# Joining the projections and the local attention of an image in one stage, with the root's steps and the loop's last copies moved

## The reference

```python
q = x @ wq.T                                   # x = layernorm(h), 16 heads of 64
k, v = split(x @ wkv.T)                        # one head each
q = _rmsnorm(_rope(q), q_norm_w)               # over the 64 features of a head
k = _rmsnorm(_rope(k), k_norm_w)
mask = (cols <= rows) & (rows - cols <= 128)
scores = where(mask, einsum(q, k) / sqrt(64), -1e30)
attn = softmax(scores)
h = h + (attn @ v).reshape(..., 16 * 64) @ wo.T
```

## Time and profile before

| | |
|---|---|
| median of 3 runs | 976.79 us (975.57 to 984.98) |
| profiled execution | 969.34 us, span of the core 967.1 us |
| mean granted clock of PE | 0.897 of full |
| busy, share of the span | PE 77%, PEld 50%, DVE 65%, ACT 46%, POOL 40% |
| first product of `project`, images 1 to 4 | 56.75, 187.00, 317.11, 449.77 us |
| first exponential of `windowed` | 98.41, 228.64, 361.16, 491.40 us |

### The profile page before, as it was taken

The page is one execution under the profiler, slowest core; times in us unless marked ns, Lnnn a source line. Parts: engine busy times, 40 slices in busy tenths (PEclk is TensorE's granted clock), DMA queues, the critical chain, the costliest instruction groups (busy, mean ns, idle before and its releaser), DMA issues. The chain is left out here.

```text
span 967.1 us, 21086 instructions
## 1 busy us (share of the span) xinstructions
PE 747.3 (77%) x8204; PEld 482.5 (50%) x8204; DVE 630.0 (65%) x1210; ACT 443.2 (46%) x1389; POOL 383.2 (40%) x432
## 2 busy tenths in 40 slices
PE   5577999887998879998769989978899965302870
PEld 5232677434775326774257744864577732201650
DVE  0378788596886787876968847676677728500890
ACT  0022899234995228991369935213666610200210
POOL 0035466254663445662646622652000000074475
PEclk9999999998999889999979999988999977655875
DMA  8144000080000620000300000008000021014200
GB/s 287 59 174 83 2 3 2 21 238 2 3 2 1 210 49 1 4 2 1 84 2 3 2 2 1 2 1 111 2 2 2 2 78 43 1 52 102 50 20 13
DMA packets 59992, 41.60 MB, mean 43 GB/s; under 512 B 51744, under 2 KB 57340, under 8 KB 59108
## 3 DMA queue, kind: packets, MB, share of 16 engines
q1 hardware_dynamic: 57446, 33.03, 13.7%
q10 hardware_dynamic: 144, 4.19, 1.1%
q0 software_dynamic: 2304, 3.04, 1.0%
HBM read 25.44 MB, written 7.15 MB: 34 GB/s over the span
## 5 line engine op out<-in xcount | busy, mean ns | idle before, releaser
L770 ACT ACTIVATE work<-ps,small,rq 128x160 f32<-128x160 f32 x512 | 243.1, 487 | 54.2 <-DVE small L719 53.7
L749 POOL TENSOR_TENSOR work<-work,small 128x512 f32<-128x512 f32 x128 | 133.3, 1042 | 138.1 <-DVE small L733 138.1
L716 DVE TENSOR_REDUCE ps<-ps 128x4 f32<-128x640 f32 x128 | 106.5, 832 | 52.4 <-PE ps L639 52.1
L727 DVE COPY pT<-ps 128x640 f32<-128x640 f32 x128 | 105.4, 823 | 8.2 <-PE ps L652 7.9
L770 ACT ACTIVATION_READ_ACCUMULATOR work<-ps,small,rq 128x1 f32 x512 | 105.2, 206 | 0.0
L1441 POOL DMA_INDIRECT sent_rows<-big,xb x32 | 30.9, 966 | 182.4 <-DVEq L1393 173.0
L639 PE MATMUL ps<-kT,big 64*128 64x160 f32 x1024 | 102.6, 322 | 0.0
L269 PE MATMUL ps<-xT,s_proj_w 64*128 64x512 f32 x288 | 78.9, 661 | 21.5 <-DVE prod L581 13.2
L669 PE MATMUL ps<-pT,vwin 128*64 128x128 f32 x1024 | 84.2, 282 | 10.6 <-ACT big L758 2.4
L609 POOL TENSOR_TENSOR big<-prod 128x1024 f32<-128x1024 f32 x28 | 66.4, 2372 | 47.5 <-DVE prod L581 47.0
L639 PEld LDWEIGHTS ps<-kT,big 64*128 64x128 f32 x1024 | 80.3, 200 | 0.4
(11 more groups left out here) (275 smaller groups left out, 1361.2 us busy)
## 6 DMA issues: line engine op xcount, KB each, us to landing
xb<-in_x SPq DMA_DIRECT2D x3, 4096.0 KB, 12.7
xb<-in_x ACTq DMA_DIRECT2D x1, 4096.0 KB, 15.1
vrem<-hl SPq DMA_DIRECT2D x64, 64.0 KB, 2.2
sent_rows<-empty_row SPq DMA_DIRECT2D x8, 325.0 KB, 10.0
s_proj_w<-in_proj_w SPq DMA_DIRECT2D x1, 1536.0 KB, 6.5
big<-sent_rows SPq DMA_DIRECT2D x5, 264.0 KB, 5.1
big<-sent_rows SPq DMA_DIRECT2D x5, 256.0 KB, 4.6
xb<-in_ffn_w SPq DMA_DIRECT2D x1, 1028.0 KB, 4.9
```

Source lines behind the costliest of these rows:

```text
L716: ch.step(v.tensor_reduce(row_max(c), ps[:, s_banks(c), 0:2 * SPAN].rearrange("p e (h k) -> p e h k", h=2), X, ALU.max))
L727: v.tensor_copy(pT[:, c % 2, :].rearrange("p (q r t) -> p r q t", r=2, t=D), ps[:, 4:6, 0:(NQ + 1) * D].rearrange("p r (q t) -> p r q t", ...
L749: g.tensor_tensor(probs[:, c % 3, :, 0:P], probs[:, c % 3, :, 0:P], bc(small[:, c % 4, 3, :], P), ALU.mult)
L770: nc.scalar.activation(probs[:, c % 3, q, :], bank[2 * (c % 2) + e][:, SPAN * hh:SPAN * hh + SPAN], ACT.Exp, bias=small[:, c % 4, 1, q:q + ...
```

## The change

The two stages of an image become one, so that only PE, DVE, ACT, POOL and SP's own semaphores stand between them; a second chain semaphore and names of their own for three counters go with it. `K_SUMS` and the steps after it move: the sums to step 4, the values to 5, the `ones` products to 7 and 8, `kT` after step 9. `STEPS` stays in order, so (8, 0) is step 16. The four transposes of the sums go to four places in `work` with no addition between; after the last, two `tensor_scalar` add the epsilon to the whole of `rq`, then the root follows. The second sums use banks 0 and 1. Token products at the end of the projections are one, and five before chunk 2. In the last three chunks DVE copies half of `pT` and ACT the other half.

```diff
-        K_SUMS, K_VALUES, K_NORMS, K_SCALED = 3, 4, (8, 9), 10
+        K_SUMS, K_VALUES, K_NORMS, K_SCALED = 4, 5, (7, 8), 9
-        SUM_BANKS = ((7, 6), (2, 3))
+        SUM_BANKS = ((7, 6), (0, 1))
-        LATE_TOKENS = 3
+        LATE_TOKENS = 1
-        STEPS[-3], STEPS[-2] = STEPS[-2], STEPS[-3]
+        VALUE_LOADS = 2 * NQ - 1 + NQ * NQ
...
-        sums_turned = pTr_own[:].rearrange("p a n -> p (a n)")
+        sums_turned = work[:].rearrange("p (k n) -> p k n", k=4)
-                v.memset(rms_eps[:], D * RMS_EPS)
... PE, project
-                        pe.wait_ge(S["prod_done"], UNITS - 1)
+                        pe.wait_ge(S["prod_done"], UNITS - 2)
... ACT, project
-                    if s == K_VALUES:
+                    if s == K_VALUES - 1:
... DVE, project
-                        ch.step(v.transpose(sums_turned, bank[SUM_BANKS[hh][w]][:]))
-                        v.sem_inc(S["q_root"], 1)
-                        ch.step(v.tensor_tensor(rq[:, w * CHUNKS // 2:(w + 1) * CHUNKS // 2, :, hh],
-                                                sums_turned.rearrange("p (c e) -> p c e", e=32)[:, :, 0:2],
-                                                rows(rms_eps[:].to_broadcast([P, 2]), CHUNKS // 2), ALU.add))
+                        v.transpose(sums_turned[:, 2 * hh + w, :], bank[SUM_BANKS[hh][w]][:]).then_inc(S["q_root"], 1)
...
                 q_sums(1)
+                v.wait_ge(S["q_root"], 4)
+                for hh in range(2):
+                    ins = v.tensor_scalar(rq[:, :, :, hh], sums_turned[:, 2 * hh:2 * hh + 2, :].rearrange(
+                        "p w (c e) -> p (w c) e", e=32)[:, :, 0:2], D * RMS_EPS, None, ALU.add)
+                ch.step(ins)
                 one_over_root(v, ch, rqflat, rqflat)
... between project and windowed
+        SHARED_FROM = CHUNKS - 3
+        def turned_half(c, r):
+            return pT[:, c % 2, :].rearrange("p (q r t) -> p r q t", r=2, t=D)[:, r]
+        def bank_of_half(r):
+            return bank[4 + r][:, 0:(NQ + 1) * D].rearrange("p (q t) -> p q t", t=D)
... PE, windowed: turn(c) and values(c) wait by this instead of pT_ready alone
+                def turned_kept(c):
+                    pe.wait_ge(S["pT_ready"], c + 1)
+                    if c >= SHARED_FROM:
+                        pe.wait_ge(S["pTr_ready"], c + 1 - SHARED_FROM)
...
+                pe.wait_ge(S["prod_done"], UNITS)
+                pe.wait_ge(S["square_done"], len(PAIR_ORDER))
+                pe.wait_ge(S["rot_done"], len(PAIR_ORDER))
                 for n in range(CHUNKS + 4):
+                    if n == 0:
+                        pe.wait_ge(S["q_root"], 4)
...
-                    if n == 4 and b + 1 < IMAGES:
-                        pe.wait_ge(S["h_ready"], 1)
+                    if n == 4:
+                        pe.wait_ge(S["x_loaded"], 16 * VALUE_LOADS)
+                        if b + 1 < IMAGES:
+                            pe.wait_ge(S["next_kept"], 1)
... DVE, windowed
-                        v.tensor_copy(pT[:, c % 2, :].rearrange("p (q r t) -> p r q t", r=2, t=D),
-                                      ps[:, 4:6, 0:(NQ + 1) * D].rearrange("p r (q t) -> p r q t", t=D)).then_inc(
-                                          S["pT_ready"], 1)
+                        if c < SHARED_FROM:
+                            v.tensor_copy(... the same ...)
+                        else:
+                            v.tensor_copy(turned_half(c, 0), bank_of_half(0)).then_inc(S["pT_ready"], 1)
... ACT, windowed
                 for c in range(CHUNKS - 4, CHUNKS):
+                    if c + 1 < CHUNKS:
+                        a.wait_ge(S["transposed"], c + 2)
+                        a.wait_ge(S["pv_done"], c)
+                        nc.scalar.activation(turned_half(c + 1, 1), bank_of_half(1), ACT.Copy).then_inc(S["pTr_ready"], 1)
                     outputs(c)
...
-            stage(lambda block: project(block, b))
-            stage(lambda block: windowed(block, b))
+            stage(lambda block: (project(block, b), windowed(block, b)))
```

More of the change, by code:

```diff
@@ L127, in program @@
         moe_b2 = sb("moe_b2", [P, E * D], BF16)
-        first_guess, rms_eps = sb("first_guess", [P, 1]), sb("rms_eps", [P, 1])
+        first_guess = sb("first_guess", [P, 1])
         ones, ones_mean, zeros = sb("ones", [P, P]), sb("ones_mean", [P, P]), sb("zeros", [P, P])
@@ L200, in program @@
             "v_dve", "kprod", "scores_done", "bias_ready", "exp_done", "scaled", "transposed",
-            "pT_ready", "pTr_ready", "tokens_kept", "tokens_turned", "pv_done", "oT_ready", "wo_done", "sums_inverted",
+            "pT_ready", "pTr_ready", "tokens_kept", "tokens_turned", "out_done", "out_kept", "next_kept", "loop_chain", "pv_done", "oT_ready", "wo_done", "sums_inverted",
             "zero_done", "slots_ready", "pool_chain", "sent", *(f"back{k}" for k in range(CHUNKS_X)), "turned_back", "hid_act",
@@ L557, in _ @@
                         n += 1
-                sp.wait_ge(S["x_loaded"], 16 * n)
+                sp.wait_ge(S["x_loaded"], 16 * VALUE_LOADS)
                 if b + 1 < IMAGES:
@@ L647, in turn @@
                     if c >= 1:
-                        pe.wait_ge(S["pT_ready"], c)
+                        turned_kept(c - 1)
                     for q in range(NQ + 1):
@@ L655, in values @@
                 def values(c):
-                    pe.wait_ge(S["pT_ready"], c + 1)
+                    turned_kept(c)
                     if c >= 1:
@@ L694, in _ @@
                                                oT[:, p, w * HALF:(w + 1) * HALF], start=(p == 0), stop=(p == PAIRS - 1))
-                ins.then_inc(S["proj_done"], 1)
+                ins.then_inc(S["out_done"], 1)
                 if b + 1 < IMAGES:
                     turn_normed(pe, 1)
-                pe.wait_ge(S["v_act"], 1)
+                pe.wait_ge(S["out_kept"], 1)
                 turn_halves(outT, 3, S["wo_done"])
@@ L702, in _ @@
             def _(v):
-                ch = Chain(v, S["dve_chain"])
+                ch = Chain(v, S["loop_chain"])
                 for n in range(CHUNKS + 3):
@@ L711, in _ @@
                         v.wait_ge(S["tokens_turned"], 1)
+                        v.wait_ge(S["h_ready"], 1)
                         v.tensor_copy(h_next.rearrange("p (w j) d -> p j w d", w=2),
-                                      bank[6][:].rearrange("p (j w d) -> p j w d", w=2, d=D)).then_inc(S["h_ready"], 1)
+                                      bank[6][:].rearrange("p (j w d) -> p j w d", w=2, d=D)).then_inc(S["next_kept"], 1)
                     if c < CHUNKS:
@@ L726, in _ @@
                             v.wait_ge(S["pv_done"], c - 1)
-                        v.tensor_copy(pT[:, c % 2, :].rearrange("p (q r t) -> p r q t", r=2, t=D),
-                                      ps[:, 4:6, 0:(NQ + 1) * D].rearrange("p r (q t) -> p r q t", t=D)).then_inc(
-                                          S["pT_ready"], 1)
+                        if c < SHARED_FROM:
+                            v.tensor_copy(pT[:, c % 2, :].rearrange("p (q r t) -> p r q t", r=2, t=D),
+                                          ps[:, 4:6, 0:(NQ + 1) * D].rearrange("p r (q t) -> p r q t", t=D)).then_inc(
+                                              S["pT_ready"], 1)
+                        else:
+                            v.tensor_copy(turned_half(c, 0), bank_of_half(0)).then_inc(S["pT_ready"], 1)
                     c = n - 1
@@ L734, in _ @@
                 if b + 1 < IMAGES:
-                    v.wait_ge(S["h_ready"], 1)
+                    v.wait_ge(S["next_kept"], 1)
                     layernorm(v, ch, h_next, xn_in_order, tmp, moe, st, TILES)
@@ L774, in _ @@
                 for c in range(CHUNKS - 4, CHUNKS):
+                    if c + 1 < CHUNKS:
+                        a.wait_ge(S["transposed"], c + 2)
+                        a.wait_ge(S["pv_done"], c)
+                        nc.scalar.activation(turned_half(c + 1, 1), bank_of_half(1), ACT.Copy).then_inc(S["pTr_ready"], 1)
                     outputs(c)
-                a.wait_ge(S["proj_done"], 1)
-                nc.scalar.activation(outT, bank[0][:], ACT.Copy).then_inc(S["v_act"], 1)
+                a.wait_ge(S["out_done"], 1)
+                nc.scalar.activation(outT, bank[0][:], ACT.Copy).then_inc(S["out_kept"], 1)
                 if b + 1 < IMAGES:
```

## The result

The changed kernel takes 935.07 us (934.44 to 941.04), the kernel before 976.18 (974.29 to 984.98): ratio 0.958, interval 0.954 to 0.962. Two more comparisons on other chips gave 0.967 (0.963 to 0.972) and 0.959 (0.957 to 0.962). The forecast was 945, 32 us less; 41 were measured. On the chip with 0.967 the two medians are 968.4 and 939.3, 29 us apart. The profiled execution took 934.44, span 932.6, against 969.34 and 967.1: the span is 34.5 less.

A forecast was written before the change was run, and what follows sets the result against it. ACT's exponentials bound the loop's steady part, no engine the projections. Terms gave 8.5 us in images 1 to 3 and 6.4 in image 4, 31.9 in all, taken off the median 976.79: 945, range 935 to 950, chance 0.66.

The forecast's parts named there:

- keys' root a pass later: Projections: one more product ahead of the keys' root and DVE's waits for projections gone; gain 2.5 us an image.
- first pair of additions: Projections: two transposes in DVE's product queue without their chained additions; gain 1.1 us an image, bounds 0.8 and 1.2.
- second pair: End of projections: second sums to rq by a transpose and two TENSOR_SCALAR; gain 1.4 us an image, bounds 0.3 and 1.7.
- order of the last steps: End of projections: (8,0) at step 16 makes the second sums one product later; minus 1.1 us an image.
- one stage: Projections to attention: no barrier, scores ready while DVE is in the root; gain 2.7 us, bounds 1.2 and 2.8.
- token products, clock: Before chunk 2: five token products at full clock, exponentials sooner; gain 2.1 us in images 1 to 3, none in 4.
- loop's end: Last three chunks: ACT's half of the pT copy stands ahead of its outputs; minus 0.2 us an image.
- the root waits for the port: Rival, end of projections: new sums wait for POOL's last rotation, 1.4 us not gained in four images; 951, chance 0.06.
- Image 4: Whole fourth image, which has no next tokens and so no token-product gain: forecast gain 6.4 us.
- the rival for a slower result: Attention loop's passes fall to 1.2 GHz, 1.7 us more per cold pass; 1% slower from 25 of 128; chance 0.03.

The follow-up runs named there:

- krate: Kernel before with only the keys' sums, values, norms and kT moved to steps 4, 5, 7, 8 and 9: 959.4 us, ratio 0.989.
- added: Changed kernel with the four chained additions behind the transposes again and none at the end: 948.6 us, ratio 0.972.
- swapped: Changed kernel with steps 15 and 16 exchanged again, (8,0) first: 940.7 us, ratio 0.963.
- best: Changed kernel with DVE alone copying pT and five unread products on PE in image 4 before chunk 2: 934.9 us, ratio 0.958.
- warm: Kernel before with unread products on PE behind the projections' token products, four an image, seven in the last: 973.1 us, ratio 0.995.
- split: Changed kernel with projections and attention again in two stages with the barrier between: 954.2 us, ratio 0.984.
- tokens3: Changed kernel with three token products ahead of the first scores and three after, still one stage: ratio 0.963.

## Why the prediction was right

The measured time lies 0.07 us inside the low edge of the range, which is luck. The mechanisms were right and their sum too (31.9 us forecast, 32.5 measured where the clock cost neither profiled execution anything in the projections), though it took for separate two terms that hang together. The rest up to 41 is, as far as the runs show, a loss of the clock that both profiled executions mostly lacked. Terms of image 1, us:

| step | forecast | measured | from |
|---|---|---|---|
| keys' root a pass later | 2.5 | 2.6 | product 11, 20.85 to 18.21 after product 0 |
| first pair of additions | 1.1 | 1.4 | 2.59 to 1.23 |
| second pair | 1.4 | 1.4 | PE's sums to the root's first step, 4.73 to 3.33 |
| order of the last steps | -1.1 | -0.9 | what the first two rows leave of product 0 to PE's second sums, 30.48 to 27.39 |
| one stage | 2.7 | 2.6 | root to reduction, 2.81 to 0.24 |
| token products, clock | 2.1 | 2.2 | 6.30 to 4.06 |
| loop's end | -0.2 | -0.1 | 5.79 to 5.88 |

Together 9.2, of which 0.2 are lost in the passes (60.66 to 60.87); the image is 9.0 us shorter, forecast 8.5. The first pair's 1.4 is above its bound of 1.2.

*Order.* The -1.1 is right as far as it goes. But I gave the second pair +1.4 as if it had nothing to do with the order. They hang together. From product 0 to the root's first step are, in image 1, all four with the keys' root moved:

| | old order | new order |
|---|---|---|
| additions behind each transpose | 32.57 (`krate`) | 32.69 (`added`) |
| two additions at the end | 32.40 (`swapped`) | 30.73 (the change), 31.64 (image 1 of `best`) |

`swapped` has a stretch at half clock here that `krate`, `added` and the change's first profile lack; 31.64 is the change with that same stretch. With the additions in place the new order gives nothing: what it costs before PE's sums it gives back behind them. With the additions gone it gives 0.8 (32.40 to 31.64), as the last rotation, for which they wait, ends 0.8 us earlier. Neither edit could be priced alone.

*Port.* The rival "the root waits for the port" is what happens with the old order, and a little with the new one. Two additions by `tensor_scalar`, with one input in SBUF, take 0.30 us in image 4 of the change, where POOL's rotation is over. They take 0.56 in images 1 to 3, where the first ends at 85.29 and the rotation at 85.23, and 2.05 in `swapped`. By this the trace agrees with the rule that I cited from the Trainium skill, SBUF — State Buffer (Who interferes with whom). That the prediction called the margin thin was right, but it was already used up: 0.26 us were lost in each of images 1 to 3. There DVE had waited 0.57 us for the last projection, where I had 0.1, and that put the last rotation back; in image 4, with no token products on PE, it waited 0.11.

*Token products.* Size right, cause half right. The gain is the clock (`warm`), and the joined stage gives it (`split`); the place of the products is worth nothing that shows (`tokens3`).

*Image 4.* Forecast 6.4, measured 5.3: its first exponential came 7.3 us earlier relative to the key's square, and then 0.6 and 1.3 were lost again in passes at half clock. That cold passes cost much was in the rival for a slower result, but for far more passes.

*The sum.* 31.9 forecast, 34.9 measured in the profiled execution, of which 2.4 are image 3's projections, which had taken 31.41. That leaves 32.5 where neither execution lost anything to the clock in the projections. What is left up to 41 I put down to the clock. Two profiles of the kernel before, 10 us apart, show it: the first was of a quick execution. With the second profile of before the images sum to 525.9 us, with the first to 517.6, after the change to 482.7: 43 or 35 less. The change did not do away with these losses, but made them smaller: from the first projection to the last square an image takes 31.5 us before, or 34.1 to 35.5 after a start at half clock, and with the change 28.6, or 29.5 to 30.7 with one or both of its stretches at half clock. Why a stage starts at half clock in one execution and not in another stays open. I had noted that the profile stood 7.4 us below the median but not asked why, and took the same gain off the median. That step, carrying a gain from one execution to the median, was the one that fell short. The runs don't show how the remaining difference between chips (968 and 977 us for the kernel before) divides.

## What to carry to other kernels

A barrier between two stages of unequal engines costs more than itself where PE runs dry before it: its clock falls, and the next stage starts on a slow PE. Joining the stages gives that back. Products that nobody reads give back a part: in `warm` they won 2 us an image behind the barrier, but held the barrier up so that the faster scores won nothing, and cost 2.3 us in image 4, where there were too many. Steps that wait for a port held by another engine are best costed by where that engine's work ends, and an order that ends it a step earlier can be worth more than the delay that it causes elsewhere. Such a pair of edits has to be costed together, and two executions compared only where the clock was the same.

## What was not expected of the hardware

Unread products paid for themselves: five of them (4.56 us of PE) before image 4's chunk 2 saved 2.7 us there. The same program had the first twelve products behind the barrier in 2.85 us or, at a granted clock of 0.50, in 4.43 from one image to the next, though PE had idled the same 1.77 us in both cases. And the clock fell to 0.50 at 186 us of a run in which PE had been busy for all of the 4 us before. No run here shows what decides either.
